# Sparse experts in float32r: three products of high and low parts, and another order of stages in the slot loop

## The reference, cut to what matters

```python
logits = jnp.einsum('th,eh->te', x, router_w)
top_vals, top_idx = jax.lax.top_k(logits, TOP_K)
top_w = jax.nn.softmax(top_vals, axis=-1)
expert = top_idx[:, 0]
weight = top_w[:, 0]
gate = jnp.einsum('th,eih->eti', x, gate_w)      # 176 x 256 per expert
up = jnp.einsum('th,eih->eti', x, up_w)
act = jax.nn.silu(gate) * up
out_e = jnp.einsum('eti,ehi->eth', act, down_w)
combine = jax.nn.one_hot(expert, e, dtype=x.dtype) * weight[:, None]
out = jnp.einsum('eth,te->th', out_e, combine)
```

## Time and profile before

| | |
|---|---|
| median of 3 runs | 383.87 us (381.69 to 384.3) |
| span of the profiled execution | 380.5 us |
| PE busy | 334.3 us, 88% |
| DVE, ACT, POOL busy | 220.0, 156.8, 100.2 us |
| mean granted TensorE clock | 0.946 |
| granted clock in 40 slices of 9.5 us, in tenths (9 is 90% or more) | 9999998588999756799999999999999999999999 |
| chain that ended last | PE 65%, DVE 14%, issue 6%, POOL 5%, ACT 5%, DMA 4% |

### The profile page before, as it was taken

One profiled execution on the slowest core, in us unless ns is written; L12 is line 12 of the kernel. 1 busy time (PEld: TensorE's weight loads), 2 busy tenths in 40 slices (PEclk: granted clock), 3 DMA queues, 4 the chain that ended last, 5 costly groups with the idle time before them and its releaser, 6 DMA issues.

```text
span 380.5 us, 4562 instructions
## 1 busy us (share of the span) xinstructions
PE 334.3 (88%) x1473; PEld 201.6 (53%) x1473; DVE 220.0 (58%) x513; ACT 156.8 (41%) x327; POOL 100.2 (26%) x154
## 2 busy tenths in 40 slices
PE   3999785969999816999989999998899989999997
PEld 1485574756666404564544654643544444445885
DVE  4345976502222347889956993993342449778911
ACT  2434341333333122136867665774874233333000
POOL 7203663520000176401342334333441001000000
PEclk9999998588999756799999999999999999999999
DMA  7997000153111114500000000000000000000011
GB/s 231 364 421 210 0 15 2 65 167 101 46 53 41 55 56 166 221 0 9 0 8 2 0 0 9 0 3 8 0 2 0 2 0 0 0 1 2 28 41 41
DMA packets 14023, 22.53 MB, mean 59 GB/s; under 512 B 2049, under 2 KB 11393, under 8 KB 13186
## 3 DMA queue, kind: packets, MB, share of 16 engines
q1 hardware_dynamic: 13234, 20.16, 15.3%
q0 software_dynamic: 768, 2.10, 1.7%
HBM read 15.96 MB, written 6.03 MB: 58 GB/s over the span
## 4 chain that ended last, share of the span: by engine, by line
PE 65%; DVE 14%; issue 6%; POOL 5%; ACT 5%; DMA 4%; SPq 1%; ACTq 0%; DVEq 0%; POOLq 0%
PE bank L241 47%; DVE mx L1216 6%; PE bank L458 5%; PE bank L426 4%; ACT region L929 3%; PE bank L429 3%; POOL x_sorted L739 2%; PE bank L257 2%; DVE stats L999 2%; PE bank L251 2%; POOL rstd L711 1%; DVE x_sb L1039 1%; PE bank L473 1%; DMA x_sb<-in_x_dram 1%; PE bank L510 1%
## 5 line engine op out<-in xcount | busy, mean ns | idle before, releaser
L929 ACT ACTIVATE region<-bank,padcol 128x512 f32<-128x512 f32 x96 | 62.4, 695 | 18.1 <-PE bank L241 17.3
L1216 DVE TENSOR_REDUCE mx<-bank 128x2 f32<-128x512 f32 (+1 forms) x96 | 61.3, 683 | 11.7 <-PE bank L429 11.4
L241 PE MATMUL bank<-xT,e_gu 128*128 128x512 f32 x128 | 57.6, 594 | 0.5 <-ACT xT L792 0.5
L775 POOL TENSOR_SCALAR_AFFINE_SELECT region<-region 128x1024 f32<-128x1024 f32 x32 | 35.0, 1094 | 81.8 <-ACT region L929 81.7
L241 PE MATMUL bank<-qst,kblk 128*128 128x512 f32 x96 | 46.1, 490 | 0.8 <-DMA qst<-nmT 0.3
L426 PE MATMUL bank<-kblk,qst 128*128 128x512 f32 x96 | 45.1, 488 | 1.7 <-ACT qst L877 0.9
L241 PEld LDWEIGHTS bank<-xT,e_gu 128*128 128x128 f32 x128 | 23.3, 190 | 25.1 <-issue 24.3
L429 PE MATMUL bank<-causb,identb 128*128 128x256 bf16 (+1 forms) x96 | 31.8, 331 | 0.0
L241 PE MATMUL bank<-e_down,region 128*128 128x256 f32 x128 | 27.8, 379 | 0.0
L707 POOL TENSOR_SCALAR veps<-mv 128x1 f32<-128x1 f32 x40 | 11.4, 284 | 62.0 <-DVE mv L1001 59.9
L241 PEld LDWEIGHTS bank<-e_down,region 128*128 128x128 f32 x128 | 24.3, 190 | 3.7 <-issue 0.5
(11 more groups left out here) (158 smaller groups left out, 543.9 us busy)
## 6 DMA issues: line engine op xcount, KB each, us to landing
e_gu<-in_e_gu_dram SPq DMA_DIRECT2D x2, 1408.0 KB, 11.9
x_sorted<-zero SPq DMA_DIRECT2D x1, 1920.0 KB, 9.1
y_sorted<-region SPq DMA_DIRECT2D x15, 128.0 KB, 1.7
x_sb<-in_x_dram SPq DMA_DIRECT2D x4, 256.0 KB, 4.2
ctxT<-in_ctxT_dram SPq DMA_DIRECT2D x2, 512.0 KB, 6.1
e_down<-in_e_down_dram SPq DMA_DIRECT2D x1, 1024.0 KB, 13.7
region<-x_sorted SPq DMA_DIRECT2D x1, 1024.0 KB, 7.3
e_gu<-in_f_gate_dram SPq DMA_DIRECT2D x1, 1024.0 KB, 4.8
```

Source lines behind the costliest of these rows:

```text
L241: return pe.matmul(dst, lhsT, rhs, start=first, stop=last)
L775: pool.affine_select(out=block, in_=block, compare_op=ALU.is_ge, fill=0.0, base=0, pattern=[[0, 2], [0, PER_GROUP], [1, P]], channel_multi ...
L929: taken(act.activation(dst, src.rearrange("p (h n) -> p h n", n=SEQ - mt * P), ACT.Exp, bias=padcol[:, key:key + 1], scale=float(HD) ** -0 ...
L1216: taken(dve.reduce_max(mx[:, b % 2, nt, quads, q, hg], src, AX), "sa")
```

## The change

The experts' weights and inputs are split on chip into a high part (the value written as float32r) and a low part (the float32 value minus that high part, written as float32r). Each float32 product becomes three float32r products in the same PSUM accumulation: high x high, low x high, high x low.

- SP's loads of the expert weights get semaphores of their own (`e_gu0`, `e_gu1`, `e_down`). The order of the loads stays. Several semaphores are merged (`routed`, `constants_set`, `pads_made`, `sel`, `caus`, `gates`, `wo0`), with the waits adapted.
- `gu_high` lies over `qhi`, `qlo` and `qst`, `down_high` over `xT`, `down2_high` in a free part of `region`; the low parts are written in place over the weights. `s_high` and `s_low` lie over `sT` and `prod`.
- DVE splits the first half of the gate/up weights (128x2816) after `padcol`, by a copy and a subtraction, ahead of the group norm. ACT makes the high part of the second half in four pieces of 128x704 in rounds 3 to 6 of the token-tile loop, DVE subtracts it in two pieces of 128x1408 after the routing. ACT copies the down weights' high parts (128x2048 and 48x2048) around `projections(0)`, DVE subtracts them between the `key_low`s.
- In a slot ACT writes `s_high` as it wrote `sT`, and DVE subtracts the low part from the same bank (`slot_low`, `slot_act_low`); the bank is free after DVE.
- In round i PE now issues gate_up(i+1), turn(i+2), act_turn(i), down(i-1).

```diff
             def slot_gate_up(i):
...
                 pe.wait_ge(sem("sx_taken"), i + 1)
+                one = bass.ds(expert, 1)
                 for t in range(KT):
-                    ins = mm(dst, sT[:, i % 2, t, :], e_gu[:, t, bass.ds(expert, 1), :].rearrange("p e n -> p (e n)"),
-                             t == 0, t == KT - 1)
+                    high = gu_high[:, t, one, :].rearrange("p e n -> p (e n)")
+                    mm(dst, s_high[:, i % 2, t, :], high, t == 0, False)
+                    mm(dst, s_low[:, i % 2, t, :], high, False, False)
+                    ins = mm(dst, s_high[:, i % 2, t, :], gu_low[:, t, one, :].rearrange("p e n -> p (e n)"),
+                             False, t == KT - 1)
...
-                mm(dst, sT[:, 2 + i % 2, 0, :], e_down[:, one, :].rearrange("p e n -> p (e n)"), True, False)
-                ready(mm(dst, sT[0:EXPERT_R, 2 + i % 2, 1, :], e_down2[:, one, :].rearrange("p e n -> p (e n)"), False, True), "sy")
...
+                for rows, t, high, low in ((slice(0, P), 0, down_high, down_low), (slice(0, EXPERT_R), 1, down2_high, down2_low)):
+                    whole = high[:, one, :].rearrange("p e n -> p (e n)")
+                    mm(dst, s_high[rows, 2 + i % 2, t, :], whole, t == 0, False)
+                    mm(dst, s_low[rows, 2 + i % 2, t, :], whole, False, False)
+                    ins = mm(dst, s_high[rows, 2 + i % 2, t, :], low[:, one, :].rearrange("p e n -> p (e n)"), False, t == 1)
+                ready(ins, "sy")
...
             slot_turn(0)
             slot_turn(1)
+            pe.wait_ge(sem("gu_split"), 4)
             expert = [slot_gate_up(0)]
             for i in range(SLOTS + 1):
+                if i + 1 < SLOTS:
+                    expert.append(slot_gate_up(i + 1))
                 if i + 2 < SLOTS:
                     slot_turn(i + 2)
-                if i + 1 < SLOTS:
-                    expert.append(slot_gate_up(i + 1))
+                if i < SLOTS:
+                    slot_act_turn(i)
+                if i == 1:
+                    pe.wait_ge(sem("down_split"), 4)
                 if i >= 1:
                     slot_down(i - 1, expert[i - 1])
-                if i < SLOTS:
-                    slot_act_turn(i)
```

On ACT and DVE:

```diff
+                if k in HIGH_AT:
+                    es = slice(2 * HIGH_AT.index(k), 2 * HIGH_AT.index(k) + 2)
+                    ins = act.activation(gu_high[:, 1, es, :], e_gu[:, 1, es, :], ACT.Copy)
...
+            loaded(act, "e_down", 2)
+            act.activation(down_high[:, :, :], e_down[:, :, :], ACT.Copy).then_inc(sem("down_split"), 1)
             projections(0)
+            act.activation(down2_high[:, :, :], e_down2[:, :, :], ACT.Copy).then_inc(sem("down_split"), 1)
             keys(0)
...
+            loaded(dve, "e_gu0")
+            dve.tensor_copy(gu_high[:, 0, :, :], e_gu[:, 0, :, :]).then_inc(sem("gu_split"), 1)
+            dve.wait_ge(sem("gu_split"), 1)
+            dve.tensor_tensor(out=gu_low[:, 0, :, :], in0=e_gu[:, 0, :, :], in1=gu_high[:, 0, :, :].bitcast(F32),
+                              op=ALU.subtract).then_inc(sem("gu_split"), 1)
...
+            dve.wait_ge(sem("gu1_high"), 1)
+            for es in (slice(0, EXPERTS // 2), slice(EXPERTS // 2, EXPERTS)):
+                dve.tensor_tensor(out=gu_low[:, 1, es, :], in0=e_gu[:, 1, es, :], in1=gu_high[:, 1, es, :].bitcast(F32),
+                                  op=ALU.subtract).then_inc(sem("gu_split"), 1)
             key_low(0)
             spread_keys(0)
-            for b in range(1, BATCH):
+            dve.wait_ge(sem("down_split"), 2)
+            dve.tensor_tensor(out=down_low[:, :, :], in0=e_down[:, :, :], in1=down_high[:, :, :].bitcast(F32),
+                              op=ALU.subtract).then_inc(sem("down_split"), 1)
+            key_low(1)
+            dve.tensor_tensor(out=down2_low[:, :, :], in0=e_down2[:, :, :], in1=down2_high[:, :, :].bitcast(F32),
+                              op=ALU.subtract).then_inc(sem("down_split"), 1)
+            for b in range(2, BATCH):
                 key_low(b)
...
+            slot_low(0)
+            slot_low(1)
             slot_product(0)
             for i in range(SLOTS + 1):
+                if i + 2 < SLOTS:
+                    slot_low(i + 2)
                 if i + 1 < SLOTS:
                     slot_product(i + 1)
+                if i < SLOTS:
+                    slot_act_low(i)
```

More of the change, by code:

```diff
@@ L170, in build_program @@
         wins = amat[:, :, :].rearrange("p h n -> p (h n)").bitcast(BF16).rearrange("p (c n) -> p c n", n=UNIT)
+        gu_high = sb_over("gu_high", [P, KT, EXPERTS, 2 * EXPERT_I], F32R, "qhi")
+        gu_low = sb_over("gu_low", [P, KT, EXPERTS, 2 * EXPERT_I], F32R, "e_gu")
+        down_high = sb_over("down_high", [P, EXPERTS, DIM], F32R, "xT")
+        down_low = sb_over("down_low", [P, EXPERTS, DIM], F32R, "e_down")
+        down2_high = sb_over("down2_high", [EXPERT_R, EXPERTS, DIM], F32R, "region", 4 * 3840)
+        down2_low = sb_over("down2_low", [EXPERT_R, EXPERTS, DIM], F32R, "e_down2")
+        s_high = sb_over("s_high", [P, 4, KT, P], F32R, "sT")
+        s_low = sb_over("s_low", [P, 4, KT, P], F32R, "prod")
         x_sorted = nc.dram_tensor("x_sorted", (SLOTS * P, DIM), F32, kind="Internal").ap()
@@ L641, in _ @@
             load(sp, "gates", gates[:, 2:4], a["g_f"])
-            load(sp, "decay", decay[:, :, :], a["decay"])
+            load(sp, "gates", decay[:, :, :], a["decay"])
             load(sp, "wg", wg[:, :, :], a["wg"])
@@ L646, in _ @@
             load(sp, "wo0", wo0[:, :, :], a["wo0"])
-            load(sp, "router", router[:, :, :], a["router"])
-            load(sp, "small", small_c[:, :], a["small"])
+            load(sp, "wo0", router[:, :, :], a["router"])
+            load(sp, "sel", small_c[:, :], a["small"])
             load(sp, "sel", sel_in, a["sel"])
@@ L653, in _ @@
             load(sp, "sel", mask_col[:, :], a["mask_col"])
-            load(sp, "tri", tri[:, :, :], a["tri"])
-            sp.wait_ge(sem("zero_set"), 1)
+            load(sp, "caus", tri[:, :, :], a["tri"])
+            sp.wait_ge(sem("constants_set"), 1)
             sp.dma_start(x_sorted.rearrange("(s p) n -> p s n", p=P),
@@ L658, in _ @@
             for t in range(KT):
-                load(sp, "e", e_gu[:, t, :, :], a["e_gu"][:, t, :, :])
-            load(sp, "e", e_down[:, :, :], a["e_down"])
-            load(sp, "e", e_down2[:, :, :], a["e_down2"])
+                load(sp, f"e_gu{t}", e_gu[:, t, :, :], a["e_gu"][:, t, :, :])
+            load(sp, "e_down", e_down[:, :, :], a["e_down"])
+            load(sp, "e_down", e_down2[:, :, :], a["e_down2"])
             load(sp, "w1", wq[:, :, :], a["wq"])
@@ L696, in _ @@
         def _(pool):
[L697 to L701, removed]
+            pool.memset(zero[:, :], 0.0).then_inc(sem("constants_set"), 1)
+            pool.memset(power[:, :], -0.5).then_inc(sem("constants_set"), 1)
+            pool.memset(vaug[:, :, :, :], 1.0).then_inc(sem("constants_set"), 1)
+            pool.memset(amat[:, :, :], 1.0).then_inc(sem("constants_set"), 1)
+            pool.wait_ge(sem("constants_set"), 2)
             chain = [0]
@@ L888, in slot_turn @@
                     act.wait_ge(sem("sg_ready"), i - 1)
-                taken(act.activation(sT[:, i % 2, :, :], src, ACT.Copy), "sx")
+                act.activation(s_high[:, i % 2, :, :], src, ACT.Copy).then_inc(sem("sx_high"), 1)
             def slot_silu(i):
@@ L908, in _ @@
                     act.wait_ge(sem("sy_ready"), i - 1)
-                act.activation(sT[:, 2 + i % 2, 0, :], src[:, 0:P], ACT.Copy)
-                taken(act.activation(sT[0:EXPERT_R, 2 + i % 2, 1, :], src[0:EXPERT_R, P:2 * P], ACT.Copy), "sa_t")
+                act.activation(s_high[:, 2 + i % 2, 0, :], src[:, 0:P], ACT.Copy).then_inc(sem("sa_high"), 1)
+                act.activation(s_high[0:EXPERT_R, 2 + i % 2, 1, :], src[0:EXPERT_R, P:2 * P], ACT.Copy).then_inc(sem("sa_high"), 1)
             def neg_turn(b):
@@ L1020, in _ @@
                     norm(0, k - 2)
[L1023 to L1024 removed]
+            loaded(dve, "gates", 3)
+            dve.wait_ge(sem("constants_set"), 4)
             for h in range(RET_HEADS):
```

68 lines of the change are left out of this document (42 added, 26 removed).

## The result

The changed kernel takes 379.06 us (median of 4 runs, 378.93 to 380.11) where the kernel before took 384.09 us beside it (4 runs, 381.69 to 384.45). The medians lie 5.0 us apart. The ratio, which goes by all runs of both kernels, is 0.989 [0.986, 0.992], so the kernel is faster by 1.1%, about 4.3 us. The profiled execution has a span of 377.3 us, where the earlier trace rows come from a span of 380.5, so this pair of traces shows 3.2 us of the difference. The runs of before have spans of 380.0 to 382.7 us: its trace is one of its faster executions.

The account below looks back on a forecast made before the run. PE was taken to bound the slot loop at 2.83 us a slot. Loop rounds -4.0, first slots -0.5, end -3.2 and late splits +0.9 sum to -6.8 from 383.87, about 377.0 us, range 372.5 to 382.0.

Parts of the forecast that it names:

- The round trip: Slot loop: gate/up, turn, high part, low part, next gate/up take 2.49 us; round taken as 2.5, gaining 4.0 us.
- PE sum of 2.46: Slot loop: PE's own work is gate/up 0.97, turns 0.49 and down 1.00, together 2.46 us.
- Rival (c): Slot loop: the path turn, high, low, gate/up exceeds the round and sets it; at 3.5 us, 389 us total; chance 0.06.
- rival (a): Slot loop: sequencer's address work and new waits keep the round at 2.83 us, about 381 us total; chance 0.14.
- The first slots: Loop start: low part adds 0.5 us, a higher clock saves about 1 us; net -0.5, at the old clock +1.5.
- The late splits: Between routing and first turn: DVE's subtractions delay keys and projections, using up PE's idle 3.02 us; cost 0 to 2.5, taken 0.9.
- rival (b): Ahead of the loop: late subtractions hold up POOL's scatters, moving the reload by up to 5 us; 380 us; chance 0.07.
- The end: Last slots: gate_up(14) to DVE's last copy falls from 8.29 to about 5.1 us, 3.2 us less through the new order.
- The split ahead of the group norm: Before the group norm: DVE's first split of 4.9 to 6.2 us fits its idle time; cost 0, at most 0.2.
- keys(0) at 73.6: Behind the routing: PE's keys move from 70.36 to 73.6 because two subtractions stand ahead of key_low(0).
- The base: Whole kernel: the difference is set against the runs' median, 383.87 us, 3.4 above the profiled span of 380.5.
- Rival (d): Slot loop: float32r of 352 dynamic columns runs no faster per record than float32; round 3.8 us, 393 total; chance 0.03.

Follow-up runs that it names:

- the two series: The changed kernel against the kernel before, measured twice: 379.06 us, ratio 0.989, then again unchanged, 380.36 us, ratio 0.992.
- the turn put first: Changed kernel with turn(i+2) moved ahead of gate_up(i+1) in the slot loop: 376.24 us, 0.983 of the kernel before.
- the reductions: Changed kernel with DVE's four late subtractions replaced by equally long maximum reductions reading one SBUF tile, those low parts left out: 377.39 us, 0.985.
- The order alone: Kernel before, float32 products and no splits, with only the new order of stages: 380.5 us, ratio 0.993.

## Why the prediction was right, and where its terms were off

It said 377.0 us (372.5 to 382.0) and faster; 379.06 was measured. In the terms, though, it said -6.8 where the medians show -5.0 and -2.5 in the two series, and the pair of traces -3.2. Direction held, and the mechanism in the loop and at the end. Two terms were too favourable, by 1.9 and 1.75 us. That the number still fell within the range owes something to the width of the range, and to a first series that came out better than the second.

**The round trip.** "Together 2.49 us" beside a PE sum of 2.46, round taken as 2.5: measured 2.64. This is the first mis-sized term, and it binds in every round, so the loop gave 2.06 us and not 4.0. (Of the missing 1.9, 0.2 lies in the kernel before: its twelve rounds took 33.74 us, 2.81 each and not 2.83.) What was short: gate/up 1.06 for 0.97, since its first matmul leads the second by 0.26; the turn to ACT 0.42 for 0.38; ACT to DVE 0.11 for 0.05. The rates of 0.162 and 0.118 us were right. PE's own sum of 2.46 came out too, but by luck: the turn put first shows 1.05 for gate/up (0.97 forecast), 1.08 for down (1.00) and 0.33 for the two turns (0.49), and the errors cancel. Rival (c) named this path as the one that could set the round; it did so, by 0.18 us and not by the 0.6 that it needed to lose.

**The sequencer, rival (a).** Costed at nothing. A round of 2.46 us with the turn first rules out that the sequencer sets 2.64 or 2.83. Some 0.1 us at the first float32r matmul of gate/up and as much at that of down (0.20 and 0.23 us to the next, where others are 0.12 apart) are there with and without a wait; whether computing the addresses takes them is open.

**The first slots.** "Net -0.5", because the clock would stay high: this step failed. The prediction had the keys and projections fill PE's hole, but they ended at 83.24, the turn came at 84.92 and the products 1.04 behind the turns, since the low parts are made in between. The clock fell as before (0.61 for 4.43 us; before 0.64 for 4.79). With the reductions, where PE worked until 84.90, it came as counted on. But the step from a filled hole to a high clock is itself not safe: with the turn first PE was idle for 0.30 us only, and the clock fell to 0.50 all the same.

**The late splits.** "Cost 0 to 2.5, taken 0.9": the first turn came 1.40 later, so the size was near, but for another reason. PE was done with the projections in time. The scatters were late, by 1.8 us in three of them: rival (b), which I had given 0.07, was the real mechanism, at about a third of its worst case. Its sign, spacings of 2 us or more, was just missed: the longest is 1.87, and three of the eight scatters started under a subtraction. I had set against it that reading 8 offsets is a small part of a scatter's 0.96 us; what counts, as the ends 0.83 to 0.86 us behind the subtractions suggest, is that it can't start. The Trainium skill, SBUF — State Buffer, section "Who interferes with whom", has the rule: a DVE instruction with two SBUF inputs contends with a GpSimd instruction that reads SBUF, a reduction doesn't, and a copy in its fast mode does. The runs agree: 1.57 and 1.89, 0.96, and 1.38 us. They don't prove the reason, since subtractions and copies also write whole tiles and the reductions don't.

Together gate_up(2) came 2.15 us later where -0.5 + 0.9 = +0.4 was forecast, the second mis-sized term.

**The end.** "About 5.1 us at full clock", -3.2: measured 5.22, -3.07. Right, the clock of down(14) included. The order alone shows it at 5.45.

**The split ahead of the group norm.** Cost 0: right, 1.61 + 3.09 = 4.7 us in the hole, 1.36 left. keys(0) at 73.6: 73.30. Both hits.

**The base.** Setting the difference against the median and not the span was right: the profiled execution of before lay below its median. How far medians differ from one series to the next (384.09, 383.54, 382.39, 382.86 for the kernel before, up to 1.7) is nearly as large as my error of 2.1. What lies behind the loop gave 0.2 us, in the 2 allowed.

**Rival (d)** fell: 0.16 us a matmul of 352 columns.

Left open: whether it is the second input or the write of a whole tile that holds up a scatter; why a copy that starts with a scatter lengthens it; what lets the clock fall when PE was hardly idle; and the best place for the splits of the down weights, of which three were tried.

## What to carry to other kernels

When work on the bounding engine gets shorter, write down the round trip beside it, hand-overs measured and not guessed; if the two come within a tenth of each other, reorder so that the producer stands ahead of the long stage. Try the new order and the new arithmetic one at a time: here the order gave 0.7% alone, and the products with their splits lost 0.6% without it. Before filling DVE's idle time with two-input operations, look at what POOL issues at that moment.

## What was not expected of the hardware

A scatter on POOL (an indirect DMA, 0.96 us) that starts under a DVE subtraction of two SBUF tiles ends 0.83 to 0.86 us behind its end; one begun with it (77.52 beside 77.49) isn't touched; under a reduction of the same length none is. A scatter of 0.96 us that begins with a float32 to float32r copy (128x2048, 1.30 us) takes 1.38.

An idle PE can cost twice. With no late work on DVE, PE idled 2.7 us and ran the next 6.75 us at a mean clock of 0.75; with reductions of no use, which push keys and projections back so that PE works until 84.90, it stayed at 2.4 GHz through the first slots, and the way from gate_up(0) to gate_up(2) was 1.27 us shorter. Of thirteen traces the clock fell there in all eight with 1.68 us or more of idle time ahead of the first turn, and in two of the five with 0.51 us or less.
